# First attention of a macaron network: 64-row tiles of TensorE, a ring of paired banks, batch ends by way of DRAM

## The reference, cut to what matters

```python
x = x + 0.5 * ffn0(layernorm(x))
x = x + attn0(layernorm(x))              # 4 batches, 16 heads of 8 features, causal softmax over 1024 tokens
x = x + 0.5 * ffn0(layernorm(x))
# attn0: q, k, v = split(x @ w_qkv.T + b_qkv); rotary embedding on q and k
#        scores = q @ k.T / sqrt(8), causal; out = softmax(scores) @ v; return out @ w_out.T + b_out
```

## Time and profile before

| | us |
|---|---|
| median of 3 runs | 3715.18 (3712.35 to 3719.55) |
| the profiled execution's own time | 3713.15 |
| its span | 3711.4 |
| attention, first to last exponential | 345.0 to 972.0, 627.0 |
| TensorE busy in the span | 3239.8 (87%) |
| VectorE, ScalarE, GpSimd busy | 2656.9 (72%), 2004.8 (54%), 588.2 (16%) |

### The profile page before, as it was taken

The page is one execution under the profiler, slowest core; times in us unless marked ns, Lnnn a source line. Parts: engine busy times, 40 slices in busy tenths (PEclk is TensorE's granted clock), DMA queues, the critical chain, the costliest instruction groups (busy, mean ns, idle before and its releaser), DMA issues. The chain is left out here.

```text
span 3711.4 us, 44165 instructions
## 1 busy us (share of the span) xinstructions
PE 3239.8 (87%) x14402; PEld 1960.8 (53%) x14402; DVE 2656.9 (72%) x6064; ACT 2004.8 (54%) x3427; POOL 588.2 (16%) x484
## 2 busy tenths in 40 slices
PE   4999999999899998779988777778799998589998
PEld 3775343443377764236544333334477776357776
DVE  5566778777355587777766888886777777777776
ACT  2444656555444445444435655543377775157776
POOL 0000000000000000000002544430023332013332
PEclk9999999999999999889999889889999999789999
DMA  2000101010000131003331000002411110011111
GB/s 78 1 24 21 39 24 36 19 44 10 22 10 1 59 97 51 1 31 97 101 105 59 1 0 1 1 17 84 135 59 46 42 31 23 0 41 35 38 47 49
DMA packets 89647, 146.27 MB, mean 39 GB/s; under 512 B 13085, under 2 KB 25565, under 8 KB 89289
## 3 DMA queue, kind: packets, MB, share of 16 engines
q1 hardware_dynamic: 89416, 143.43, 12.5%
HBM read 134.02 MB, written 9.34 MB: 39 GB/s over the span
## 5 line engine op out<-in xcount | busy, mean ns | idle before, releaser
L358 POOL TENSOR_TENSOR norm_rstd<-norm_rstd,minus_half 128x4 f32<-128x4 f32 x144 | 174.3, 1211 | 2210.7 <-DVE norm_rstd L349 2208.2
L952 ACT ACTIVATE main_tiles<-banks 128x512 f32<-128x512 f32 (+3 forms) x768 | 356.9, 490 | 246.3 <-PE banks L940 166.3
L2189 ACT ACTIVATE main_tiles_r<-banks,feature_cols 128x512 fp32r<-128x512 f32 x512 | 353.2, 690 | 190.4 <-PE banks L228 168.5
L821 DVE TENSOR_REDUCE gate_scratch<-banks 128x1 f32<-128x512 f32 (+3 forms) x608 | 367.1, 655 | 122.4 <-PE banks L771 94.7
L2197 DVE TENSOR_TENSOR main_tiles_r<-main_tiles,main_tiles_r 128x512 fp32r<-128x512 f32 x512 | 383.4, 764 | 69.9 <-ACT main_tiles L2190 68.4
L226 PE MATMUL banks<-normed_pairs,moe_weights 128*128 128x512 f32 x800 | 409.2, 512 | 18.4 <-ACT main_tiles L2190 7.1
L2190 ACT ACTIVATE main_tiles<-banks,feature_cols 128x512 f32<-128x512 f32 x512 | 350.2, 684 | 0.0
L227 PE MATMUL banks<-normed_pairs,moe_weights 128*128 128x512 f32 x800 | 318.2, 398 | 0.0
L228 PE MATMUL banks<-normed_pairs,moe_weights 128*128 128x512 f32 x800 | 317.8, 397 | 0.0
L2234 POOL TENSOR_TENSOR normed<-normed,main_tiles 128x512 f32<-128x512 f32 x128 | 217.7, 1701 | 538.7 <-DVE main_tiles L2223 538.7
L226 PE MATMUL banks<-main_tiles_r,moe_weights 128*128 128x512 f32 x640 | 266.5, 416 | 28.3 <-DVE main_tiles_r L2197 26.4
(11 more groups left out here) (333 smaller groups left out, 6788.3 us busy)
## 6 DMA issues: line engine op xcount, KB each, us to landing
main_tiles<-gates_d SPq DMA_DIRECT2D x400, 256.0 KB, 3.3
weight_staging<-in_w SPq DMA_DIRECT2D x33, 256.0 KB, 3.7
parts_d<-bf_parts SPq DMA_DIRECT2D x48, 128.0 KB, 1.8
q_stacks<-parts_d SPq DMA_DIRECT2D x192, 32.0 KB
k_stacks<-parts_d SPq DMA_DIRECT2D x192, 32.0 KB
x_res<-in_x_t SPq DMA_DIRECT2D x8, 256.0 KB, 3.4
out_x<-x_res SPq DMA_DIRECT2D x8, 256.0 KB, 3.7
rope<-in_rope SPq DMA_DIRECT2D x1, 1024.0 KB
```

Source lines behind the costliest of these rows:

```text
L821: eng.tensor_reduce(o, bank[:, 0:per * (k1 - k0)].rearrange("p (n c) -> p n c", n=per), AX.X, ALU.max).then_inc(s.ring_free)
L952: eng.activation(weight_tile(e)[:, 0:C - q0], psum[:, 4 + e % 2, 0:C - q0], ACT.Exp, scale=HD ** -0.5).then_inc(s.at_exp)
L2189: eng.activation(pair_3(j)[0], psum[:, 2 + j % 2, :], ACT.Relu, bias=bias)
```

## The change

- q and k stacks are read as 64 rows: head h uses partitions 0 to 63 or 64 to 127 by its parity, with `tile_position=(64 * side, 0)`. In the search the matmuls of an even and an odd head follow each other into two different banks. A mask, since 64 rows of the identity cover half the partitions of the output, becomes two matmuls of 128 and 64 columns on its 64 rows; a second constant tile with the two 64-row halves swapped is loaded at the start by four more transfers.
- The ring has two slots of two banks (1 and 2, 3 and 4). A search item is 20 instructions of VectorE a group where there were 38, each over both banks. The projection and its rotated partner are one item.
- Scores use banks 5 and 6, from the 25th exponential on also bank 0, up to the last 32. Weight tiles are 12. The rows use bank 7 alone, and ScalarE, no longer VectorE, copies it out.
- The six norms of batches 1 to 3 move into the first FFN (the last of them to its end) and keep their results in eight tiles; the odd batches' values have a tile of their own, which GpSimd sets to one.
- GpSimd does the three passes that split q and k.
- Batch end: found tiles go to DRAM, the denominators come back as 128 by 64, VectorE takes that reciprocal, which goes to DRAM and comes back spread over the heads' features; the numerators come back as one tile, GpSimd multiplies, `out` follows. The eight `den` and eight `num` items are gone.
- Planned times: 27 us a group, searches 43 us ahead, projections 94 us ahead, stacks 53 us ahead; the second FFN's first chunk 14 us behind the last group, where it was 32.

```diff
+    v2_t = at("v_rows_odd", [P, 8, 176], F32, spare_a)
+    found_d = nc.dram_tensor("found_d", [NB, 2, NH, 32, C], F32, kind="Internal").ap()
+    rec_d = nc.dram_tensor("rec_d", [NB, 2, NH, C], F32, kind="Internal").ap()
...
+    def add_mask(eng, o, side, mask):
+        for half in range(2):
+            m = (matb if half == side else matb_swapped)[64 * side:64 * side + 64, :]
+            c0, c1 = (64 * half, TILE) if mask == 1 else (0, 64 * half + 64)
+            z = eng.matmul(o[:, c0:c1], m[:, 0:P], m[:, mask * P + c0:mask * P + c1], start=False, stop=half == 1,
+                           tile_position=(64 * side, 0))
+        return z
...
     def plan_ffn(i):
-        begin = ffn_b[i] - 40.0 if i % NC_ == 0 else ffn_b[i] - FFN_US - 16.0
+        begin = ffn_b[i] - (28.0 if i else 40.0) if i % NC_ == 0 else ffn_b[i] - FFN_US - 16.0
...
-    GROUP_US = 42.0
+    GROUP_US = 27.0
+    SEARCH_LEAD = GROUP_US + 16.0
+    PROJ_LEAD = 2 * GROUP_US + 40.0
...
+    num_t, recs_t = wlt[:, 0, :], wlt[:, 1, :]
+    at_tiles = [wlt[:, 0, :], wlt[:, 1, :], xn_t[:, 0, :], xn_t[:, 1, :], xn_t[:, 2, :], nat_t[:, 4, :], nat_t[:, 5, :],
+                nat_t[:, 6, :]]
+    for c in range(NC_):
+        at_ = ffn_b[c + 1] + 27.0 if c < NC_ - 2 else ffn_b[NC_ - 1] + (17.0, 36.0)[c - NC_ + 2]
...
+    SEARCH = [(i, 0, 2, 0, (i + 1) * TILE) for i in range(2)] + \
+        [(i, j, 1, 0, (i + 1) * TILE) for i in range(2, 4) for j in range(2)]
+    SEARCH += [n for i in range(4, 8) for n in [(i, j, 1, 0, C) for j in range(2)] +
+               [(i, j, (2, 2, 1, 1)[i - 4], C, (i + 1) * TILE) for j in range(0, 2, (2, 2, 1, 1)[i - 4])]]
...
+        slot = 0 if key[:2] in (("proj", 0), ("out", NB - 1)) or n == 0 else 1 - ring_slot[-1]
...
-    def ring_bank(n):
-        return psum[:, 1 + n % 3, :]
+    def ring_bank(n, side=0):
+        return psum[:, 1 + 2 * ring_slot[n] + side, :]
...
     def q_of(g, h, j0, j1):
-        return qs_t[:, g % 3, h // 2, j0:j1]
+        return qs_t[64 * (h % 2):64 * (h % 2) + 64, g % 3, h // 2, j0:j1]
...
     def pe_ring(eng):
-            if n >= 3:
-                eng.wait_ge(s.ring_free, n - 2)
+            if ring_before[n] is not None:
+                eng.wait_ge(s.ring_free, ring_before[n] + 1)
...
+                for j in range(per):
+                    for side in range(2):
+                        h = 2 * (j0 + j) + side
+                        z = eng.matmul(ring_bank(n, side)[:, j * width:(j + 1) * width], q_of(g, h, i * TILE, (i + 1) * TILE),
+                                       k_of(g, h, k0, k1), start=True, stop=not diag, tile_position=(64 * side, 0))
                     if diag:
+                        for side in range(2):
+                            z = add_mask(eng, ring_bank(n, side)[:, (j + 1) * width - TILE:(j + 1) * width], side, 1)
...
             else:
                 _, b, half = key
-                eng.wait_ge(s.at_acc, 2 * (4 * b + 3) + half + 1)
-                for g in range(4):
-                    c0 = MATS[kind] + 96 - 32 * g
-                    z = eng.matmul(bank, matf[:, c0:c0 + P], found(g, half), start=g == 0, stop=g == 3)
+                eng.wait_ge(s.num_rec, 2 * b + half + 1)
+                z = eng.matmul(bank, w0n[:, N0["o"]:N0["o"] + P], num_t, start=True, stop=True)
...
             elif kind == "search":
+                eng.tensor_reduce(o.rearrange("p (n s) -> p s n", s=2)[:, :, j0:j0 + per],
+                                  psum[:, b0:b0 + 2, 0:per * (k1 - k0)].rearrange("p s (n c) -> p s n c", n=per), AX.X,
+                                  ALU.max).then_inc(s.ring_free)
...
-            elif kind == "den":
-                eng.reciprocal(fin, bank).then_inc(s.ring_free)
-            elif kind == "num":
-                eng.tensor_tensor(fin, bank, fin, ALU.mult).then_inc(s.ring_free)
...
-    def dve_turned(eng):
+    def pool_turned(eng):
...
     def sp_stacks(eng):
-            yield group_at[g] - 62.0
+            yield group_at[g] - 2 * GROUP_US + 1.0
...
+    score_at, score_before, score_used = [], [], {5: -2, 6: -1}
+    for e in range(AT_EXPS):
+        if e == 24:
+            score_used[0] = -1
+        if e == AT_EXPS - 32:
+            SCORES_IN_0 = score_used.pop(0) + 1
+        bank = min(score_used, key=score_used.get)
...
+    WEIGHT_TILES = 12
...
     def pe_scores(eng):
-                if e >= 2:
-                    eng.wait_ge(s.at_exp, e - 1)
+            if score_before[e] >= 0:
+                eng.wait_ge(s.at_exp, score_before[e] + 1)
...
+            side, o = h % 2, psum[:, score_at[e], :]
+            z = eng.matmul(o[:, 0:C - q0], k_of(g, h, i * TILE, (i + 1) * TILE), q_of(g, h, half * C + q0, half * C + C),
+                           start=True, stop=not diag, tile_position=(64 * side, 0))
+            if diag:
+                z = add_mask(eng, o[:, 0:TILE], side, 2)
+            z.then_inc(s.at_score)
...
     def pe_rows(eng):
-                    if a >= 2:
-                        eng.wait_ge(s.at_acc, a - 1)
+                if a:
+                    eng.wait_ge(s.at_acc, a)
...
-    def dve_acc(eng):
+    def act_found(eng):
+                eng.activation(found(g % 4, half), psum[:, 7, :], ACT.Copy).then_inc(s.at_acc)
...
+    def sp_found(eng):
+                eng.dma_start(found_d[b, half, 4 * (g % 4):4 * (g % 4) + 4], found(g % 4, half)).then_inc(found_out[half], 16)
+                if g % 4 < 3:
+                    continue
...
+                eng.dma_start(den_t, found_d[b, half, :, HD, :].rearrange("h (j c) -> h j c", c=64)).then_inc(s.den_in, 16)
...
+                eng.dma_start(num_t, found_d[b, half, :, 0:HD, :]).then_inc(s.num_in, 16)
+                yield when + 9.0
+                eng.wait_ge(s.den_rec, k + 1)
+                eng.dma_start(rec_d[b, half].rearrange("h (j c) -> h j c", c=64), rec_t).then_inc(s.rec_out, 16)
+                yield when + 12.2
+                eng.wait_ge(s.rec_out, 16 * (k + 1))
+                eng.dma_start(recs_t, rec_d[b, half][:, None, :].broadcast_to([NH, HD, C])).then_inc(s.rec_in, 16)
...
+            eng.reciprocal(rec_t, den_t).then_inc(s.den_rec)
...
+            eng.tensor_tensor(num_t, num_t, recs_t, ALU.mult).then_inc(s.num_rec)
...
-    ffn_b += [group_at[GROUPS] + 32.0 + FFN_US * i for i in range(NC_)]
+    ffn_b += [group_at[GROUPS] + 14.0 + FFN_US * i for i in range(NC_)]
```

More of the change, by code:

```diff
@@ L747, in pe_ring @@
             if kind == "proj":
-                _, b, half, side, table = key
+                _, b, half, side = key
                 if n == 0:
                     eng.wait_ge(s.at_in, 128)
-                if side == 0 and table == 0:
+                if side == 0:
                     eng.wait_ge(*normed(("at", 2 * b + half)))
-                c0 = N0[("q", "qs", "k", "ks")[2 * side + table]]
-                z = eng.matmul(bank, w0n[:, c0:c0 + P], wlt[:, half, :], start=True, stop=True)
+                for table in range(2):
+                    c0 = N0[("q", "qs", "k", "ks")[2 * side + table]]
+                    z = eng.matmul(ring_bank(n, table), w0n[:, c0:c0 + P], at_tiles[2 * b + half], start=True, stop=True)
             elif kind == "v":
@@ L862, in act_turned @@
         for t, b, half, side, when in turns():
-            yield when + 4.0
+            yield when + 5.0
             eng.wait_ge(s.at_full, t + 1)
@@ new lines, in pe_rows @@
+    def pe_rows(eng):
+        for e, g, when, half, i, h, q0, diag in weighed_heads():
+            if h < 3:
+                continue
+            yield when + (4.4 if i == 0 else 2.6)
+            a = 2 * g + half
+            if i == 0:
+                if a:
+                    eng.wait_ge(s.at_acc, a)
+                else:
+                    eng.wait_ge(s.ffn_h, 8 * NC_)
+                if g % 4 == 0 and half == 0:
+                    eng.wait_ge(s.ring_free, ring_no["v", g // 4, 1] + 1)
+            eng.wait_ge(s.at_exp, e + 1)
+            for k in range(4):
+                c9 = 9 * (4 * (g % 4) + k)
+                y = eng.matmul(psum[32 * k:32 * k + 32, 7, q0:C], v_of(g // 4)[:, i, c9:c9 + 32],
+                               weight_tile(e - 3 + k)[:, 0:C - q0], start=i == 0, stop=i == TPC * (half + 1) - 1,
+                               tile_position=(0, 32 * k))
+            y.then_inc(s.at_pv)
```

283 lines of the change are left out of this document (151 added, 132 removed).

## The result

The changed kernel takes 3625.04 us (median of 4 runs, 3619.12 to 3627.71) beside 3715.05 of the kernel before on the same chip: ratio 0.9754, with a 95% interval of [0.9737, 0.9771]. That is 90 us less, where 165 less were forecast. The profiled execution took 3623.62 us, its span is 3620.6.

What follows compares the result with a forecast made beforehand. TensorE was taken as the bound, with VectorE and ScalarE waiting for it. From 3713 us: attention -150, behind it -19, ahead +4, giving 3548, as median 3550; own range 3495 to 3620, with two rivals inside 3495 to 3625 (0.82).

Steps and rivals of the forecast that it cites:

- (b): Rival at the search starts: stacks come 4 us late, each start blocks TensorE 3 us, 3598 in all; chance 0.14.
- (d): Rival at batch ends: round trips hold up SyncE or the ring, four times 10 us, 3590 in all; chance 0.05.
- Search and scores: TensorE in a plain group: paired row tiles bring search to 6.2 us for 9.6 and scores to 8.4 for 9.6.
- The 32 with a mask can't pair: Plain group's masked score matmuls: a head's mask stands between them, so they keep 10,240 columns, 4.3 us.
- (a): Rival in the attention: row tiles don't overlap or pairs seldom start together; plain group 36 us, 3684 in all; chance 0.10.
- (c): Rival at the mask matmuls: exposed 98 ns weight loads add 12.5 us a plain group, 3748 in all, slower; chance 0.04.
- The three engines are then ... closer than before ... I take 1.7: Plain group: engines at 25.8, 22 and 24 us, TensorE's waits 1.7 for 3.8, so 27.5 us a group.
- With a microsecond of waits 13 for 28.6: Once-a-batch work in the attention: 13 us for 28.6, counted three times, less 2 at the last groups.
- A clock of 1.00 in the attention: Attention: no clock stated for it; the prediction only said the clock drops in the gates as it does now.
- Together 4 us more: Ahead of the attention: start 2 us, six norms 5 (7 with waits), searches give back 3; bounds 0 to 12.
- Behind the attention: From last scores to the second FFN's first hidden product: 17 us for 36, 19 less; bounds 12 to 22.
- Queues and round trips: SyncE's transfers and batch ends: stacks level, at most 1 us a group lost; round trips of some 13 us covered.

## Why the prediction was right, and where it was off

The direction and the mechanism held: TensorE's load fell, and the time came out of plain groups and batch ends. The size did not: 90 us for 165. The measured 3625 lies above the forecast's own range, which ended at 3620, and on the very edge of the one that ended at 3625; that one was the wider for rivals (b) and (d), and neither came true. That the time still falls there is luck. Step by step:

**Search and scores: right in size.** Pairs in 0.22 us; tiles worth 4.1 us a plain group for the 4.4 of the floor. Masks cost 0.08 us for two heads, not 0.14. "The 32 with a mask can't pair" was wrong: 3 pairs with masks stand in the plain group, such as the one at 591.14, whose four masks follow it. Rival (a), no overlap, fell. Rival (c), slower by exposed weight loads, fell with the four masks in 0.08 us, each with weights of its own, two of them on each half of the rows. The Trainium skill's rule in "TensorE: Matmul & The Clock Gate", The mechanism, that a load overlaps a running matmul only when its row group differs, would lay the load bare at least at the second mask of each half; at the 98 ns of the earlier trace rows that is more than the 0.08 us of all four, so this trace does not agree with it.

**"The three engines are then ... closer than before ... I take 1.7" of waits: failed in size.** The plain group takes 28.9, not 27.5, and 16 times 1.4 is 22 of the 40 us missing in the attention. TensorE's records show 2.9 us idle. The step lumped the third score bank into the waits and gave it no price of its own, though it is worth as much as the tiles in a plain group, because two banks tie TensorE to ScalarE.

**"With a microsecond of waits 13 for 28.6", three times, less 2: failed in size.** It is 15.6 to 16.0 in the middle batches, but the first batch pays 17.7 where it paid 14.3 before. The sum took three batch ends (37 us) and the kernel has 55, 18 more. The next batch's projections stand in the first batch too. The last group, counted as the shortest, takes 32.5 us as bank 0 leaves it (28.6 with the bank).

**A clock of 1.00 in the attention, assumed without a word: failed.** The prediction speaks of the clock behind the attention alone. The 24 us at 0.50 lie in boundary groups, in groups with projections and in the last one, and cost 8 to 12 us by the estimate above, of the 40 missing in the attention; they are part of the 18 at the batch ends. In the first FFN TensorE runs at 0.50 for another 17 us, where it did not before. In single profiles it can be far more. The first group of the changed kernel, and the same group of the one that keeps bank 0 to the end:

```profile
380.00:417.40 37.40, 32.62 (x320) 13.36 (x321) 26.46 (x40) 23.82 (x54) 9.33 (x8) 0.95 0.06 19
```

```profile
373.90:414.90 41.00, 37.05 (x320) 15.30 (x324) 26.81 (x40) 24.04 (x55) 9.35 (x8) 0.79 0.05 17
```

The same 320 matmuls take 3.6 us more at 0.79.

**"Together 4 us more" ahead of the attention: failed, +35.** By the ends of the FFN's chunks: start 2.7; chunks 2 to 5 8.8 more; chunks 6 and 7 8.8 more; the last 14.1 more (22.4 to 36.5); 0.6 to the exponential. The six norms were costed by TensorE's turns alone, at 5 us and 7 with waits; in the kernels with two score banks they put off the first exponential by 11.5 (360.8 to 372.3). What was left out is that the turn back waits for VectorE, 1.7 to 1.9 us in five of the norms, with the FFN's products behind it; spread, chunks 2 to 5 take 1.0 us more than before, and chunks 6 and 7 take 3.0 more. Two of the five waits are those of the first batch's norms, which were only brought forward: with the six back in the attention, chunks 2 and 3 still take 5.2 us more than before, and the first exponential comes 15.8 later. The term was sized for six norms and left these two out. In the last chunk stand the searches of the first two groups: 33 reductions are done before the first exponential, 1.65 groups of 20, where 42 were done before, 1.1 groups of 38. At that pace VectorE is late (5.1 us of waits of L812 for L862), and the granted clock of the stretch was 0.86, where before it was 1.00 (320.4 to 343.6). With the reductions halved the chunk takes 30.1 us, with the six norms back 32.2. I called this a gain of 3. Some 6 of the 35 seem to belong to this one profile: four kernels with the same work in the first FFN have their first exponential at 372 to 375 (a fifth at 378). Their first group is longer in turn, 39.7 to 42.6 us for 37.5, with TensorE at 0.50 for 17 us or more of it, so that their second group begins only 2 to 3 us sooner than the 417.4 here.

**Behind the attention: right**, 18.3 us less for 19.

**Queues and round trips: right.** Rival (b), late stacks, fell: no search waits for a transfer in the whole attention. Rival (d) fell too; apart from GpSimd, whose waits hold nobody up, the round trip is waited for by VectorE's short reciprocals alone:

```profile
L1083 DVE RECIPROCAL gate_scratch<-gate_scratch 128x64 f32<-128x64 f32 x7 | 3.8, 549 | 2.6 <-DMA gate_scratch<-found_d 2.6
```

**The parts don't add up.** Undone one at a time, the tiles (40), the third bank (67), the batch ends (74) and GpSimd's passes (8), less the norms (9), make 180 us, twice the gain of all together. Some parts unlock others, as the table of banks and rows has it, and a kernel with a part undone can also lose more to the clock (65 and 55 us at 0.50 without the third bank and without the new batch ends, for 24); the forecast, a sum of terms, has no place for either.

## What to carry to other kernels

Where two engines hand two banks back and forth, price the third bank before anything that makes one of them faster: here all of the change without it gave 0.9 us a plain group, and the tiles alone 4.1 with it. When work moves into a stage where TensorE is full, cost every wait that stands in TensorE's order behind the moved step, not the step's own columns, and space its steps so that the other engines finish first (17 us here for one number). Count what comes once a batch from the sum over all groups, not from one boundary times the number of boundaries. Read the granted clock of a group before a difference of one or two microseconds in it is put down to anything else.

## What the hardware showed that I had not expected

- Masks on 64-row tiles: four matmuls of 128 and 64 columns, weights changed for each, in 0.08 us for two heads, against 0.06 for one head's one mask of 128 columns on all rows. The two halves of the rows work side by side down to this size.
- With tiles of 64 rows TensorE's granted clock falls to 0.50 now and then in the attention (10 to 74 us of it in eleven kernels), and never in the three kernels with 128 rows.
- The granted clock of the last chunk of the first FFN. Windows of the changed kernel from 338.0 to 340.7, from there to 343.0, and to 346.0:

```profile
338.00:340.70 2.70, 0.94 (x14) 0.38 (x10) 2.34 (x4) 0.00 (x0) 0.00 (x0) 0.99 0.00 0
340.70:343.00 2.30, 1.42 (x3) 1.16 (x4) 1.87 (x3) 0.00 (x0) 0.00 (x0) 0.50 0.03 7
343.00:346.00 3.00, 3.00 (x9) 2.32 (x8) 0.00 (x0) 0.00 (x0) 0.00 (x0) 0.50 0.00 0
```

TensorE stood for VectorE twice (0.8 and 1.8 us, the second until 341.6; busy 0.94 of 2.7) and ran at 0.50, which is 1.2 GHz, for at least 5.3 us, 4.4 of them busy; in the kernel with bank 0 kept to the end, whose first FFN does the same work, the last chunk took 33.6 us at 0.95 and ran at 1.00 from 340 to 360. What the fall costs here is at most half of those 4.4 us, and it may be part of the 6 us that seem to be this profile's own.
- A found tile of 256 KB written to DRAM lands in 2.0 us (2.0 to 3.4) and its numerators are back in 3.4, with TensorE free meanwhile; the return through memory takes the place of 7.1 us of its matmuls a half batch.
